# First expert layer of an eight-sublayer network on one core: GpSimd makes the first comparison of each half of the ternary weights, VectorE copies the turned row in 16 of 39 tiles

## The chip, the cores and the metric

The program runs on one core of one Trainium2 chip. The metric is the device time of one execution in microseconds, the median of several runs; lower is better. Engines: PE is TensorE, DVE VectorE, ACT ScalarE, POOL GpSimd, SP SyncE (it only issues DMAs here).

## The reference, cut to what matters

The network has four layers, each an attention and a feed-forward sublayer with a gated residual, over 2048 tokens (32 x 64) of width 256. Two sublayers matter here. The feed-forward sublayer of layer 0 is a mixture of 8 experts, of which each token takes two, beside a shared one. That of layer 1 is another mixture of 8 experts, whose weights are made ternary, matrix by matrix:

```
# layer 0, routed experts (inner width 176)
h = einsum('th,ehi->eti', x, w1); g = einsum('th,ehi->eti', x, w3)
y_all = einsum('eti,eih->eth', silu(h) * g, w2)

# layer 1, each of gate_w, up_w, down_w (512 x 256) of each of 8 experts
def weight_quant(w):
    scale = 1.0 / maximum(mean(abs(w)), EPS)
    return clip(round(w * scale), -1.0, 1.0) / scale
```

The quantised value is -1, 0 or 1 times the mean of the absolute values: 1 where w is above half the mean, -1 where it is below minus half the mean. The kernel makes it as (w > mean/2) - (w < -mean/2).

## The kernel before, in words

Layer 0's routed experts (`sorted_experts`, called by `layer0_experts`) sort the token rows by expert into 39 tiles of 128 rows (NT = 39) and then run one loop over the tiles, software-pipelined over three of its steps. All five engines run their own instruction stream, written out by hand and tied together by semaphores. Everything is computed in f32 split into a high and a low part (fp32r), so each product is three matmuls. In step j:

- SP fetches the row tile (`got`, ring of 7) and, by the table `LOADS_AT`, the raw weights of layer 1's experts (`tern_raw`, three slots).
- PE (`tensor`): up-projection of tile j (L1584, 6 matmuls into bank 2 or 3), turning of tile j-1's activation (L1598), turning of the rows of tile j+2 (`tensor_in`, L1542, into bank 0 or 1), down-projection of tile j-2 (L1610).
- ACT (`scalar`): silu of tile j (L1320), high part of the turned activation j-1 (L1326), high part of the turned row j+2 (`scalar_in`, L1343, `f_xT_hi`), the output y of tile j-2 (L1334, `f_y`), then `beside.scalar`.
- DVE (`vector`): silu times the second product, tile j (L1462, `f_act`), low part of the turned activation j-1 (L1467), then `vector_low(j+2)`: the places (L1418) and the low part of the turned row (L1419, `f_xT_lo`), then `beside.vector`.
- POOL (`gpsimd`): the scatter of y to its rows in memory, an indirect DMA for each tile (L1284), once s.out says that y is there.

Beside this loop runs the making of layer 1's ternary weights for four experts (`make_ternary`); each expert has three matrices of two halves, 128 x 512 each. It is spread over the tiles by `FIRST, PERIOD = 6, 7`: expert i has seven tiles from tile 6 + 7 i on. ACT sums absolute values in the first four of them (`beside_scalar`, L689: an activation and a read-out of the accumulator; two halves, one, two, one). In the fifth, PE adds the sums over partitions (`beside_tensor`, L700, four small matmuls into the bank that the turning uses next) and DVE makes mean, `above` and `below` (`beside_scale`, L706 to L709). From the sixth on, DVE makes the halves (`beside_vector`), two instructions each:

```
if x == 0:
    dve.tensor_scalar(to, src, below[:, m, n:n + 1], None, ALU.is_lt).then_inc(below_there, 1)
else:
    dve.wait_ge(below_there, 6 * i + 2 * m + h + 1)
    dve.scalar_tensor_tensor(to, src, above[:, m, n:n + 1], to, ALU.is_gt, ALU.subtract).then_inc(tern, 1)
```

(L717 and L720; `SHARES` gives five tiles one half each and splits the sixth half over the last two tiles.) The twelve halves of the later experts are made in layer 1's attention by the same functions.

When the loop is over, SP waits until the last scatters have landed, loads a bias row (L1715) and then fetches the outputs back (L1232) for the sum into the residual.

Of the kernel before, what the change touches and what calls it, by code (L numbers as in the profile page):

```python
# [8 lines left out]
ALU = mybir.AluOpType  # L9
# [10 lines left out]
P = 128  # L20
D = 256
DC = D // P
# [26 lines left out]
def build_program(nc, io):  # L49
    ctx = ExitStack()  # L50
    with ctx:
# [41 lines left out]
        bank = [ctx.enter_context(nc.psum_tensor(f"bank{i}", [P, 512], F32)) for i in range(8)]  # L93
# [558 lines left out]
        def make_ternary():  # L652


            w = Names()
# [3 lines left out]
            size, total, chain, below_there, tern = whole_sems[1:6]  # L659
# [3 lines left out]
            slot_of = (0, 1, 2, 0, 2, 0, 1, 2)  # L663
# [48 lines left out]
            def vector(dve, i, op):  # L712
# [5 lines left out]
                else:  # L718
                    dve.wait_ge(below_there, 6 * i + 2 * m + h + 1)
                    dve.scalar_tensor_tensor(to, src, above[:, m, n:n + 1], to, ALU.is_gt, ALU.subtract).then_inc(tern, 1)  # L720

            FIRST, PERIOD = 6, 7
            SHARES = ((0, 2), (2, 4), (4, 6), (6, 8), (8, 10), (10, 11), (11, 12))

# [13 lines left out]
            def beside_scale(dve, j, to):  # L738
                i, x = divmod(j - FIRST, PERIOD)
                if 0 <= i < 4 and x == 4:  # L740
                    vector_scale(dve, i, to)

            def beside_vector(dve, j):
                i, x = divmod(j - FIRST - 5, PERIOD)
                if 0 <= i < 4:
                    for op in range(*SHARES[x]):
                        vector(dve, i, op)

# [19 lines left out]
            w.beside_sync, w.beside_scalar, w.beside_tensor, w.beside_vector = beside_sync, beside_scalar, beside_tensor, beside_vector  # L768
            w.beside_scale = beside_scale
            w.behind_scalar = behind_scalar  # L770
# [3 lines left out]
        ternary = make_ternary()  # L774
# [272 lines left out]
        def sorted_experts(name, sublayer, split, turn, gate, before, done, g, experts, top, inner, shared_inner, router_args, at,  # L1047
# [23 lines left out]
                s.here0, s.here1, s.here2, s.here3, s.in_ps, s.hi, s.lo, s.up, s.silu, s.act, s.turn_ps, s.ahi, s.alo, s.down, s.out,  # L1071
                s.back0, s.back1, s.back2, s.back3, s.stat, s.acc
            ) = early.of("here0 here1 here2 here3 in_ps hi lo up silu act turn_ps ahi alo down out "
                         "back0 back1 back2 back3 stat acc")
            s.here, s.back = (s.here0, s.here1, s.here2, s.here3), (s.back0, s.back1, s.back2, s.back3)
# [158 lines left out]
            def gpsimd(pool):  # L1234
# [44 lines left out]
                for j in range(NT):  # L1279
                    pool.wait_ge(s.lo, j + 1)  # L1280
                    if j == 0:
                        pool.sem_clear(late.range)
                    pool.wait_ge(s.out, j + 1)
                    pool.indirect_dma_start(g.outputs, bass.IndirectOffsetOnAxis(ap=dest[:, j:j + 1], axis=0),  # L1284
                                            y_out[:, j % OUT_RING, :], None).then_inc(gone[j % OUT_RING], 16)

            def scalar(act):
# [27 lines left out]
                for j in range(NT + 2):  # L1315
# [5 lines left out]
                    if 1 <= j <= NT:  # L1321
# [4 lines left out]
                        act.activation(aT_hi[0:KR, i % 2].rearrange("p c n -> p (c n)"), bank[4 + i % 2][0:KR, 0:DC * P], ACT.Copy).then_inc(s.ahi, 1)  # L1326
                    if j + 2 < NT:
                        scalar_in(act, j + 2)
# [87 lines left out]
            def vector_low(dve, j):  # L1416
                dve.wait_ge(s.hi, j + 1)
                dve.tensor_copy(dest[:, j:j + 1], got[:, j % IN_RING, D:D + 1])  # L1418
                dve.tensor_tensor(xT_lo[:, j % 2].rearrange("p c n -> p (c n)"), bank[j % 2][:, 0:DC * P],  # L1419
                                  xT_hi[:, j % 2].rearrange("p c n -> p (c n)").bitcast(F32), ALU.subtract).then_inc(s.lo, 1)  # L1420
# [197 lines left out]
        def layer0_experts(before, done):  # L1618
# [48 lines left out]
            beside.behind_scalar = ternary.behind_scalar  # L1667
            beside.scale = ternary.beside_scale
            steps_at = {3: ("which",), 5: ("powers",), 7: ("series",), 9: ("weights",)}
# [2210 lines left out]
```

## Time and profile before

| | |
|---|---|
| median of 3 runs | 1132.63 us (1128.28 to 1133.96) |
| profiled execution | 1128.05 us, span 1126.2 us, mean granted clock 0.919 |
| busy share of the span | PE 81%, DVE 69%, ACT 54%, POOL 39% |
| loop over the 39 tiles | from 148.7 us (first L1584) to 240.6 us (end of the last scatter) |

How to read it: the engines' times overlap, so busy shares don't add up; what matters is which engine others wait for in each stretch. Times of single instructions in the trace are from start to end, and on DVE and ACT the next instruction can start some hundredths of a us before the end of the one ahead. PEld is TensorE's weight load. "<-" behind idle time names what ended it.

### The profile page before, as it was taken

To read this page: it belongs to the slowest core of one execution; us is meant where nothing else is said; L and a number is where in the kernel's file an instruction comes from. 1 tells how busy PE (TensorE), PEld (TensorE's weight loads), DVE (VectorE), ACT (ScalarE), POOL (GpSimd) and SP (SyncE) were. 2 spreads that over 40 slices of the span, in tenths; PEclk is the share of its full clock that TensorE was granted. 3 is DMA by queue.
4 is the path that set the end of the run, shared out by engine and by line. 5 is a ranking of instruction groups with operands and counts; after the bars stand their busy time and mean duration, and the time that the engine had idled before them with its cause. 6 is when DMAs were issued, how large, how long until landed. Compare 5 with 4: busy or idle time off the path is not lost. (4 is left out here: it accounts for less than half of the span.)

```text
span 1126.2 us, 20364 instructions
## 1 busy us (share of the span) xinstructions
PE 914.9 (81%) x5861; PEld 679.7 (60%) x5861; DVE 776.1 (69%) x2020; ACT 605.4 (54%) x1385; POOL 444.4 (39%) x518
## 2 busy tenths in 40 slices
PE   5867989968999776778779899977998898995187
PEld 4556779966777443444455556645777686763165
DVE  5756648867887687777768887656945354339987
ACT  3663347755443386777836566566134543433385
POOL 3176624440000104756436536531046666534400
PEclk9988989989999796999979999989999998985599
DMA  9954557765200031222190002011042532351001
GB/s 265 175 163 123 173 177 215 214 216 194 71 20 1 1 85 31 65 60 62 62 300 19 10 11 65 1 49 55 1 161 89 148 101 80 85 195 58 0 20 57
DMA packets 95971, 109.19 MB, mean 97 GB/s; under 512 B 14269, under 2 KB 85842, under 8 KB 95874
## 3 DMA queue, kind: packets, MB, share of 16 engines
q1 hardware_dynamic: 84162, 76.76, 23.7%
q0 software_dynamic: 11712, 31.20, 8.7%
q8 instruction: 53, 0.87, 0.3%
q14 instruction: 44, 0.36, 0.1%
HBM read 73.89 MB, written 34.03 MB: 96 GB/s over the span
## 5 line engine op out<-in xcount | busy, mean ns | idle before, releaser
L3125 POOL DMA_INDIRECT f_got<-f_tokens,f_places x54 | 54.9, 1016 | 61.9 <-DVE f_places L946 45.7
L3131 POOL DMA_INDIRECT f_outputs<-f_y,f_places x54 | 54.8, 1015 | 47.7 <-ACT f_y L3188 32.8
L3257 DVE TENSOR_TENSOR f_act<-f_silu,bank 128x256 f32<-128x256 f32 x54 | 22.7, 421 | 71.6 <-ACT f_silu L3174 51.5
L1284 POOL DMA_INDIRECT f_outputs<-f_y,f_places x39 | 41.7, 1068 | 56.1 <-ACT f_y L1334 32.7
L2087 POOL DMA_INDIRECT f_got<-f_tokens,f_places x39 | 41.2, 1057 | 55.3 <-DVE f_places L946 37.8
L2522 POOL TENSOR_TENSOR work<-work 128x512 f32<-128x512 f32 x32 | 32.7, 1052 | 71.3 <-ACT work L2572 71.3
L2095 POOL DMA_INDIRECT f_outputs<-f_y,f_places x39 | 38.7, 993 | 36.9 <-ACT f_y L2150 28.0
L2670 DVE TENSOR_REDUCE work<-bank 128x8 f32<-128x512 f32 x64 | 43.4, 679 | 12.4 <-PE bank L2768 12.2
L3347 PE MATMUL bank<-f_rhi,f_xT_hi 128*128 x108 | 44.3, 411 | 3.7 <-DVE f_xT_lo L3198 3.1
L2328 PE MATMUL bank<-tern,f_xq 128*128 x156 | 46.7, 428 | 0.5
L2674 DVE TENSOR_TENSOR work<-bank,work 128x512 f32<-128x512 f32 x64 | 44.3, 692 | 3.7 <-ACT work L2634 1.6
L2634 ACT ACTIVATE work<-work 128x512 f32<-128x512 f32 x64 | 40.3, 629 | 8.9 <-DVE work L2674 8.7
L2238 DVE TENSOR_TENSOR f_once<-f_relu,bank 128x512 f32<-128x512 f32 x39 | 26.7, 684 | 26.5 <-ACT f_relu L2131 18.4
L2809 PE MATMUL bank<-ident,work 128*128 128x128 f32 x256 | 42.8, 291 | 1.1 <-ACT work L2634 1.1
L3347 PE MATMUL bank<-f_rhi,f_xT_lo 128*128 x108 | 43.6, 404 | 0.0
L3347 PE MATMUL bank<-f_rlo,f_xT_hi 128*128 x108 | 43.5, 403 | 0.0
L3174 ACT ACTIVATE f_silu<-bank 128x256 f32<-128x256 f32 x54 | 20.9, 388 | 41.3 <-PE bank L3347 33.4
L258 POOL TENSOR_SCALAR ln_ve<-ln_mv 128x2 f32<-128x2 f32 x16 | 3.2, 199 | 101.2 <-DVE ln_mv L1484 93.2
L2802 PE MATMUL bank<-work 128*32 128x128 f32 x512 | 27.7, 288 | 18.8 <-ACT work L2637 18.6
L2637 ACT ACTIVATE work<-bank 128x512 f32<-128x512 f32 x64 | 38.0, 593 | 8.9 <-PE bank L2809 8.7
L223 DVE BATCH_NORM_STATS2 ln_stat<-resid 128x6 f32<-128x256 f32 x96 | 36.7, 414 | 3.6 <-DMA resid<-in_x 0.8
L3373 PE MATMUL bank<-f_rhi,f_aT_hi 128*128 x108 | 36.0, 333 | 3.9 <-DVE f_aT_lo L3261 2.2
(557 smaller groups left out, 3165.6 us busy)
## 6 DMA issues: line engine op xcount, KB each, us to landing
f_back<-f_outputs SPq DMA_DIRECT2D x21, 256.0 KB, 4.8
f_back<-f_outputs SPq DMA_DIRECT2D x10, 512.0 KB, 6.0
f_got<-f_sorted SPq DMA_DIRECT2D x39, 129.0 KB
f_sorted<-clear_row SPq DMA_DIRECT2D x1, 4992.0 KB, 28.5
raw<-in_L_ffn_w SPq DMA_DIRECT2D x24, 176.0 KB
tern_raw<-in_L_ffn_gate_w SPq DMA_DIRECT2D x8, 512.0 KB
tern_raw<-in_L_ffn_up_w SPq DMA_DIRECT2D x8, 512.0 KB
tern_raw<-in_L_ffn_down_w SPq DMA_DIRECT2D x8, 512.0 KB
```

What stands on the lines that cost most here:

```text
L1284: pool.indirect_dma_start(g.outputs, bass.IndirectOffsetOnAxis(ap=dest[:, j:j + 1], axis=0), y_out[:, j % OUT_RING, :], None).then_inc(gon ...
L2087: pool.indirect_dma_start(got[:, j, :], None, tokens, bass.IndirectOffsetOnAxis(ap=sorter.token[:, j:j + 1], axis=0)).then_inc(sent[j % FL ...
L2095: pool.indirect_dma_start(outputs, bass.IndirectOffsetOnAxis(ap=sorter.dest[:, j:j + 1], axis=0), y_out[:, j % OUT_RING, :], None).then_in ...
L2328: mm = pe.matmul(bank[b + j % 2][:, :], xq[:, j % 2, c, :], weights[:, ds(at + (m * MAT + c * I), I)], start=c == 0, stop=c == DC - 1)
L2634: act.activation(prob[:, x % 2, :], score[:, x % 2, :], ACT.Exp, scale=HD ** -0.5).then_inc(s.exp, 1)
L2637: act.activation(probT[:, (x - 1) % 2, :], TURN[:, :], ACT.Copy).then_inc(s.probT, 1)
L2670: dve.tensor_reduce(top[:, x % 2, :], got, AX.X, ALU.max).then_inc(s.top, 1)
L2674: dve.tensor_tensor(score[:, x % 2, :].rearrange("p (g k) -> p g k", g=GROUPS), got, top[:, x % 2, :].unsqueeze(2).to_broadcast([P, GROUPS ...
L2809: tp = pe.transpose(TURN[:, c * P:(c + 1) * P], prob[:, x % 2, c * P:(c + 1) * P], ident[:, :])
L3125: pool.indirect_dma_start(got[:, j % GATHERS, :], None, tokens, bass.IndirectOffsetOnAxis(ap=sorter.token[:, j:j + 1], axis=0)).then_inc(s ...
L3131: pool.indirect_dma_start(outputs, bass.IndirectOffsetOnAxis(ap=sorter.dest[:, j:j + 1], axis=0), y_out[:, j % OUT_RING, :], None).then_in ...
L3347: mm = pe.matmul(bank[2 + j % 2][:, :], x[:, j % 2, c, :], w[:, ds(where[j] + c * UP_COLS, UP_COLS)], start=n == 0, stop=n == 3 * DC - 1)
```

## The change

For the four experts of the loop, the first comparison (w below) moves from DVE to POOL (`gpsimd_below`, L725 of the changed kernel), one half behind each of six scatters, in POOL's steps 9 + 7 i to 14 + 7 i. It is written with a second operation, times 1.0. DVE makes the second comparison in its steps 12 + 7 i to 17 + 7 i (before: 11 + 7 i to 17 + 7 i), and waits there for POOL's. In the four tiles of each seven in which ACT sums weights, the high part of the turned row is no longer ACT's but DVE's: a copy out of the bank, a wait on that copy, then the places and the low part as before. A new semaphore `s.hi_taken` counts these copies. The later experts' halves, made in layer 1's attention, stay with DVE.

```diff
--- before.py
+++ after.py
@@ -719,8 +719,13 @@
                     dve.wait_ge(below_there, 6 * i + 2 * m + h + 1)
                     dve.scalar_tensor_tensor(to, src, above[:, m, n:n + 1], to, ALU.is_gt, ALU.subtract).then_inc(tern, 1)
 
+            def gpsimd_below(pool, i, m, h):
+                n = expert(i)
+                pool.wait_ge(chain, 3 * i + 3)
+                pool.tensor_scalar(half(w.tern[:, n], i, m, h), half(raw_m[slot_of[i]], i, m, h), below[:, m, n:n + 1], 1.0,
+                                   ALU.is_lt, ALU.mult).then_inc(below_there, 1)
+
             FIRST, PERIOD = 6, 7
-            SHARES = ((0, 2), (2, 4), (4, 6), (6, 8), (8, 10), (10, 11), (11, 12))
 
             def beside_scalar(act, j):
 
@@ -740,11 +745,20 @@
                 if 0 <= i < 4 and x == 4:
                     vector_scale(dve, i, to)
 
+            def beside_gpsimd(pool, j):
+                i, x = divmod(j - FIRST - 3, PERIOD)
+                if 0 <= i < 4 and x < w.PER:
+                    gpsimd_below(pool, i, x // 2, x % 2)
+
             def beside_vector(dve, j):
-                i, x = divmod(j - FIRST - 5, PERIOD)
-                if 0 <= i < 4:
-                    for op in range(*SHARES[x]):
-                        vector(dve, i, op)
+                i, x = divmod(j - FIRST - 6, PERIOD)
+                if 0 <= i < 4 and x < w.PER:
+                    vector(dve, i, 2 * x + 1)
+
+            def taken_by_vector(j):
+
+                i, x = divmod(j - 2 - FIRST, PERIOD)
+                return 0 <= i < 4 and x < 4
 
             LOADS_AT = {6: (0, 0), 7: (0, 1), 8: (0, 2), 11: (1, 0), 13: (1, 1), 15: (1, 2), 18: (2, 0), 20: (2, 1), 22: (2, 2),
                         24: (3, 0), 26: (3, 1), 28: (3, 2), 36: (4, 0), 37: (4, 1), 38: (4, 2)}
@@ -766,7 +780,7 @@
 
             w.sync, w.scalar, w.tensor, w.vector_scale, w.vector = sync, scalar, tensor, vector_scale, vector
             w.beside_sync, w.beside_scalar, w.beside_tensor, w.beside_vector = beside_sync, beside_scalar, beside_tensor, beside_vector
-            w.beside_scale = beside_scale
+            w.beside_scale, w.beside_gpsimd, w.taken_by_vector = beside_scale, beside_gpsimd, taken_by_vector
             w.behind_scalar = behind_scalar
             return w
 
@@ -1069,9 +1083,9 @@
             s = Names()
             (
                 s.here0, s.here1, s.here2, s.here3, s.in_ps, s.hi, s.lo, s.up, s.silu, s.act, s.turn_ps, s.ahi, s.alo, s.down, s.out,
-                s.back0, s.back1, s.back2, s.back3, s.stat, s.acc
+                s.back0, s.back1, s.back2, s.back3, s.stat, s.acc, s.hi_taken
             ) = early.of("here0 here1 here2 here3 in_ps hi lo up silu act turn_ps ahi alo down out "
-                         "back0 back1 back2 back3 stat acc")
+                         "back0 back1 back2 back3 stat acc hi_taken")
             s.here, s.back = (s.here0, s.here1, s.here2, s.here3), (s.back0, s.back1, s.back2, s.back3)
             was_sent, was_gone = scattered[-1][0:4], scattered[-1][4:]
             scattered.append(tuple(was_sent[r] + 16 * K * len(range(r, TILES, LINES)) * (r < LINES) for r in range(4))
@@ -1283,6 +1297,7 @@
                     pool.wait_ge(s.out, j + 1)
                     pool.indirect_dma_start(g.outputs, bass.IndirectOffsetOnAxis(ap=dest[:, j:j + 1], axis=0),
                                             y_out[:, j % OUT_RING, :], None).then_inc(gone[j % OUT_RING], 16)
+                    beside.gpsimd(pool, j)
 
             def scalar(act):
                 act.wait_ge(*before)
@@ -1324,7 +1339,7 @@
                         if i >= 2:
                             act.wait_ge(s.down, i - 1)
                         act.activation(aT_hi[0:KR, i % 2].rearrange("p c n -> p (c n)"), bank[4 + i % 2][0:KR, 0:DC * P], ACT.Copy).then_inc(s.ahi, 1)
-                    if j + 2 < NT:
+                    if j + 2 < NT and not beside.taken_by_vector(j + 2):
                         scalar_in(act, j + 2)
                     if j >= 2:
                         i = j - 2
@@ -1414,7 +1429,13 @@
                 dve.tensor_tensor(rlo[:, here], staging[:, n % STAGES, :], rhi[:, here].bitcast(F32), ALU.subtract).then_inc(p.lo_late, 1)
 
             def vector_low(dve, j):
-                dve.wait_ge(s.hi, j + 1)
+                if beside.taken_by_vector(j):
+                    dve.wait_ge(s.in_ps, j + 1)
+                    dve.wait_ge(s.up, j - 1)
+                    dve.tensor_copy(xT_hi[:, j % 2].rearrange("p c n -> p (c n)"), bank[j % 2][:, 0:DC * P]).then_inc(s.hi_taken, 1)
+                    dve.wait_ge(s.hi_taken, sum(beside.taken_by_vector(x) for x in range(j + 1)))
+                else:
+                    dve.wait_ge(s.hi, sum(not beside.taken_by_vector(x) for x in range(j + 1)))
                 dve.tensor_copy(dest[:, j:j + 1], got[:, j % IN_RING, D:D + 1])
                 dve.tensor_tensor(xT_lo[:, j % 2].rearrange("p c n -> p (c n)"), bank[j % 2][:, 0:DC * P],
                                   xT_hi[:, j % 2].rearrange("p c n -> p (c n)").bitcast(F32), ALU.subtract).then_inc(s.lo, 1)
@@ -1665,7 +1686,7 @@
             beside.bias_sync = lambda sp: layer1_weights.load_bias(sp)
             beside.context_sync = lambda sp: layer1_weights.load_context(sp, range(RING))
             beside.behind_scalar = ternary.behind_scalar
-            beside.scale = ternary.beside_scale
+            beside.scale, beside.gpsimd, beside.taken_by_vector = ternary.beside_scale, ternary.beside_gpsimd, ternary.taken_by_vector
             steps_at = {3: ("which",), 5: ("powers",), 7: ("series",), 9: ("weights",)}
             return sorted_experts("f0", 1, 0, 0, gates[:, 4:5], before, done, sorted0, EXPERTS, 2, L0_I, SHARED, (True, io["L0_ffn_gate_w"]),
                                   at, load_shared, load_routed, steps_at, beside)
```

DVE's rows in two steps of the loop that have both kinds of ternary work, before (L1462 is the product with silu, L1467, L1418 and L1419 as above, L717 and L720 the two comparisons):

```order
L1462 TENSOR_TENSOR f_act<-f_silu,bank 128x176
L1467 TENSOR_TENSOR f_aT_lo<-bank,f_aT_hi 88x256
L1418 CAST f_places<-f_got 128x1
L1419 TENSOR_TENSOR f_xT_lo<-bank,f_xT_hi 128x256
L717 TENSOR_SCALAR tern<-tern_raw_50,tern_table 128x512
L720 SCALAR_TENSOR_TENSOR tern<-tern_raw_50,tern_table,tern 128x512
```

and of the changed kernel, in a step in which ACT sums weights:

```order
L1483 TENSOR_TENSOR f_act<-f_silu,bank 128x176
L1488 TENSOR_TENSOR f_aT_lo<-bank,f_aT_hi 88x256
L1435 CAST f_xT_hi<-bank 128x256
L1439 CAST f_places<-f_got 128x1
L1440 TENSOR_TENSOR f_xT_lo<-bank,f_xT_hi 128x256
L720 SCALAR_TENSOR_TENSOR tern<-tern_raw_50,tern_table,tern 128x512
```

The number of rows is the same: the comparison behind the low part is gone, the copy L1435 stands in front of it.

POOL's rows in the same stretch of the changed kernel, where the comparisons of one expert end and those of the next begin (L1298 is the scatter; before, it stands there 39 times and nothing else):

```order
L1298 DMA f_outputs<-f_y,f_places 9088x256
L725 TENSOR_SCALAR tern<-tern_raw_51,tern_table 128x512
L1298 DMA f_outputs<-f_y,f_places 9088x256 x2
L725 TENSOR_SCALAR tern<-tern_raw_52,tern_table 128x512
L1298 DMA f_outputs<-f_y,f_places 9088x256
```

Six scatters of seven have a comparison behind them, the seventh has none.

## Rows read from the trace of the kernel before

**Rows 1.** The page: span, busy time of each engine.

```profile
span 1126.2 us, 20364 instructions
PE 914.9 (81%) x5861; PEld 679.7 (60%) x5861; DVE 776.1 (69%) x2020; ACT 605.4 (54%) x1385; POOL 444.4 (39%) x518
```

**Rows 2.** Windows: busy us, instructions in brackets, clock, DMA share, GB/s.

```profile
175.00:190.00 15.00, 14.38 (x109) 13.93 (x109) 13.24 (x42) 11.57 (x37) 7.06 (x7) 1.00 0.73 227
```

**Rows 3.** Timeline of one ordinary tile: start, duration, engine, line, operation.

```profile
176.64 0.33 DVE L1462 TENSOR_TENSOR f_act<-f_silu,bank 128x176 f32<-128x176 f32 x1
...
177.17 0.33 PE L1584 MATMUL bank<-f_rhi,f_xT_hi 128*128 x1
...
177.29 0.41 DVE L1419 TENSOR_TENSOR f_xT_lo<-bank,f_xT_hi 128x256 fp32r<-128x256 f32 x1
...
177.37 0.47 ACT L1334 ACTIVATE f_y<-bank,f_got 128x256 f32<-128x256 f32 x1 [0.29 <-issue]
...
177.62 0.47 DVE L717 TENSOR_SCALAR tern<-tern_raw,tern_table 128x512 bf16<-128x512 f32 x1
...
178.12 0.75 DVE L720 SCALAR_TENSOR_TENSOR tern<-tern_raw,tern_table,tern 128x512 bf16<-128x512 f32 x1
178.13 0.38 PE L1598 MATMUL bank<-ident,f_act 128*88 128x128 f32 x2
...
178.60 1.11 POOL L1284 DMA_INDIRECT f_outputs<-f_y,f_places  x1 [1.04 <-ACT f_y L1334]
...
179.28 0.33 PE L1584 MATMUL bank<-f_rhi,f_xT_hi 128*128 x1
...
179.44 0.41 DVE L1419 TENSOR_TENSOR f_xT_lo<-bank,f_xT_hi 128x256 fp32r<-128x256 f32 x1
...
179.48 0.48 ACT L1334 ACTIVATE f_y<-bank,f_got 128x256 f32<-128x256 f32 x1 [0.29 <-issue]
```

**Rows 4.** Timeline around one sum of the weights (L700).

```profile
185.62 0.33 PE L1584 MATMUL bank<-f_rhi,f_xT_hi 128*128 x1
...
186.03 0.47 ACT L1334 ACTIVATE f_y<-bank,f_got 128x256 f32<-128x256 f32 x1
...
186.91 0.20 ACT L689 ACTIVATION_READ_ACCUMULATOR tern<-tern_raw 128x1 f32 x1
...
187.37 0.58 PE L700 MATMUL bank<-tern_table,ones 128*128 128x3 f32 x4 [0.62 <-ACT tern L689]
...
188.98 0.33 PE L1584 MATMUL bank<-f_rhi,f_xT_hi 128*128 x1
```

**Rows 5.** Waits in 145 to 240 us: total us, times, longest us.

```profile
PEld bank L700 <- issue: 3.4, 4, 0.9
```

**Rows 6.** GpSimd's groups by shape, 512 wide: busy us, mean ns.

```profile
L2522 POOL TENSOR_TENSOR work<-work 128x512 f32<-128x512 f32 x32 | 32.7, 1052 | 71.3 <-ACT work L2572 71.3
L2941 POOL TENSOR_TENSOR f_rlo<-f_staging,f_rhi 128x512 fp32r<-128x512 f32 x21 | 26.6, 1295 | 0.0
...
L2937 POOL CAST f_rhi<-f_staging 128x512 fp32r<-128x512 f32 x21 | 12.6, 635 | 0.0
```

**Rows 7.** Timeline of GpSimd: two scatters in the loop.

```profile
183.03 1.47 POOL L1284 DMA_INDIRECT f_outputs<-f_y,f_places  x1 [1.17 <-DVE f_xT_lo L1419]
184.94 0.96 POOL L1284 DMA_INDIRECT f_outputs<-f_y,f_places  x1 [0.44 <-DVE f_xT_lo L1419]
```

**Rows 8.** Timeline of the loop's end and of what follows.

```profile
235.20 0.96 POOL L1284 DMA_INDIRECT f_outputs<-f_y,f_places  x1 [0.48 <-issue]
...
235.91 0.74 DVE L720 SCALAR_TENSOR_TENSOR tern<-tern_raw,tern_table,tern 128x512 bf16<-128x512 f32 x1
...
236.65 0.42 DVE L1467 TENSOR_TENSOR f_aT_lo<-bank,f_aT_hi 88x256 fp32r<-88x256 f32 x1
...
238.22 0.47 ACT L1334 ACTIVATE f_y<-bank,f_got 128x256 f32<-128x256 f32 x1 [0.60 <-PE bank L1610]
...
239.64 0.96 POOL L1284 DMA_INDIRECT f_outputs<-f_y,f_places  x1 [0.30 <-issue]
...
242.12 0.28 SPq L1715 DMA_DIRECT2D ctx_sb<-in_L_xattn_bg  x1
```

## The prediction

> **What bounds the kernel now.** I read the page first [rows 1]: one core, span 1126.2 us, TensorE busy 81% of it. That share is an average over many stages, so it says little about this change, which touches one loop of 39 tiles. The table of windows comes next [rows 2]: inside that loop TensorE is busy 14.38 of 15 us at full granted clock and VectorE 13.24 of 15, so both are nearly full, ScalarE less, GpSimd half empty. The timeline of one ordinary tile [rows 3] tells which of the two sets the pace. The first up-projection matmul of a tile starts at 177.17 and that of the next at 179.28: 2.11 us, with no gap in TensorE. VectorE's same instruction (L1419) comes at 177.29 and 179.44, a step of 2.15: it is full too, but what it makes is early. Its product L1462 ends at 176.97 and TensorE takes it at 178.13, 1.16 us later. So VectorE may fall 1.1 us behind before TensorE notices. TensorE is the bound, at 2.11 us a tile, and no edit on another engine can shorten that.
>
> What can be shortened are four places where TensorE does wait: the tile in which it adds up ScalarE's sums of the weights (L700). There a tile takes 188.98 - 185.62 = 3.36 us instead of 2.11 [rows 4], 1.25 us more. The table of waits gives the four together: the weight loads of L700 sat idle for 3.4 us [rows 5], 0.85 each. The other 0.4 of each is the four small matmuls themselves, which stay.
>
> **The change, part by part.** (1) ScalarE loses the copy of the turned row (L1343) in the four tiles in which it also sums weights. That seems to be four copies off a queue that is late, but only what stands ahead of the last sum without another wait behind it counts. The order on ScalarE is silu, copy, copy of the row, y (L1334), sums. y waits for TensorE's down-projection: in an ordinary tile it starts 179.48 - 177.17 = 2.31 us behind the tile's first matmul [rows 3]. In the fourth sum tile, which starts 2.11 ahead of 185.62, so at 183.51, y starts at 186.03 [rows 4], 2.52 behind. So at most 0.21 us of ScalarE's lateness is left at y; from there the last sum, its read-out (186.91) and L700 (187.37) follow rigidly. Removing four copies brings 0.21 us a time, four times 0.84 us. The rest of the wait stays, about 0.6 us a time.
>
> (2) VectorE gets 16 copies 128x256 out of PSUM, each followed by a wait on itself. No such copy on VectorE stands in the trace; the nearest row is L1419 of the same shape and with the same PSUM source, 0.41 us [rows 3]. A cast with one source can be somewhat shorter and can hardly be longer than it by more than the wait: 0.3 to 0.5, I take 0.42. It loses 24 comparisons L717 that hold it for 0.50 us each (177.62 to 178.12 [rows 3]). A copy tile thus costs VectorE 2.15 - 0.50 + 0.42 = 2.07 us, an ordinary ternary tile 1.65. Both are below 2.11; VectorE stops being full, and since TensorE had 1.16 us in hand this brings nothing by itself.
>
> (3) GpSimd gets 24 comparisons 128x512, f32 in and bf16 out, one behind each of six scatters out of seven. This is the unknown price. The trace has three rows of that width on GpSimd [rows 6]: a cast with one input 0.635 us, a two-input operation 1.052, a two-input subtraction to another type 1.295. The new one has one tensor input, so it is nearest to the cast; I take 0.70 and keep 0.64 and 1.30 as ends. The Trainium skill (GPSIMD Engine Reference, Engine selection) says that one-input operations run there at roughly line rate; the cast agrees with it, while its section on pitfalls of Q7 kernels puts bodies that compare and select at up to twice that unless they are unrolled, by which the price would be nearer to the second row.
>
> A scatter takes 0.96 us when nothing disturbs it, and back to back it comes 0.30 behind the one ahead [rows 7, 8]. With about 0.10 to start the comparison, GpSimd's cycle is 0.96 + 0.30 + 0.10 + p = 1.36 + p. With p = 0.70 that is 2.06, just under 2.11: it keeps up. The tipping point is p = 0.75.
>
> (4) VectorE's second comparison (L720) now waits for GpSimd, and behind it in VectorE's order stands all that TensorE needs. By rows 3: y ends at 177.84, its scatter starts at 178.60 and would end at 179.56; the comparison would be done at about 180.4. VectorE reaches its place in the next tile at 179.44 + 0.33 + 0.42 = 180.2. It waits 0.2 us, inside the 1.16 that TensorE has in hand. SP's waits on finished weights ask for groups that end in the same tiles as before, and SP runs seven tiles ahead.
>
> (5) The end of the loop has no such cover. The last comparison sits behind scatter 35, which starts at 235.20 [rows 8]: done at 236.16 + 0.10 + 0.70 = 236.96. VectorE's last L720, now at 235.91, moves to about 237.07; L1467 of the last tile follows 0.67 behind, at 237.74 instead of 236.65: 1.09 later. The last down-projection, the last y and the last scatter hang on it. Of this 0.19 was hidden: y of the last tile ends at 238.69 and would have let its scatter start 0.76 later, at 239.45, while the queue let it start at 239.64. The end of that scatter releases SP (242.12) and so the next stage. Cost: 0.90 us.
>
> Sum: -0.84 + 0.90 = +0.06 us, no change. For the profiled execution (1128.05 us) this gives 1128.1; the median of the runs shown is 1132.63, 4.6 above it, so the forecast is **1132.7 us**. A measurement of this kernel can tell about 0.5%, 5.7 us, from no change. The bounds of case A: with p = 0.64 and a copy of 0.3 the tail costs 0.85 and the sum is 0.0; if in the stretched tiles VectorE's fullness was the cause, some tenths come back: -0.5. With p = 0.9 GpSimd slips 0.15 a tile and the tail grows by 0.2 + 5 x 0.15 to 1.85: +1.0.
>
> **The rivals.**
>
> B, slower: GpSimd becomes the bound of the ternary tiles. With p = 1.05 its cycle is 2.41, 0.30 over the tile. The first wait of VectorE is 0.6, five tiles later it is 2.1, less the 1.16 in hand: TensorE loses 0.95 in a period, of which up to the 0.64 left of the wait at L700 may swallow a part, so 0.3 to 0.95, three times; the fourth period ends in the tail, which costs 1.09 + 0.35 + 1.5 - 0.19 = 2.75. With the gain of 0.84 taken off: +2.8 to +4.8, say +3.8. With p = 1.30 the same sum gives a slip of 0.55 a tile, three times 1.8 to 2.4, a tail of 4.3: +9 to +11. It decides from p of about 0.9 on. For it: the two-input rows, and that a comparison is not a cast. Against it: one input only.
>
> C, faster: the whole wait at L700 goes, 3.4 us, 1129.2. It needs y of the fourth sum tile not to hang on TensorE; rows 4 say that it does, so only if several sums slip ahead of it. The tail must cost nothing too.
>
> D, slower by contention: a scatter which starts while L720 runs takes longer. The one at 183.03 took 1.47 us instead of 0.96 [rows 7], with L720 running; the one at 178.60, which had L720 beside it for its first 0.27 us only [rows 3], took 1.11. L720 will now start just when GpSimd goes on to its next scatter, in 24 tiles. If each cost the full 0.51, the cycle is 2.57, as with p = 1.21 in B: +6 to +8, 1139.7. Against it: the scatter waits for y anyway, and by then half of L720 is over, so a cost of 0.15 to 0.3, which lands in A's upper part. The Trainium skill (SBUF, Who interferes with whom) states that a VectorE instruction with two SBUF inputs and a GpSimd instruction that reads SBUF exclude one another for the whole instruction, and that single-source VectorE operations from SBUF can do so too. The longer scatters over L720 agree. By that rule L720 would also hold back a comparison on GpSimd that meets it, which only happens once VectorE is a tile late.
>
> **How the numbers follow.** A 0.62, B 0.20, C 0.08, D 0.10. A spans 1132.2 to 1133.7 before the scatter of medians; C reaches to 1129.2, the middle of B and the lower part of D to 1139. The range 1129.0 to 1139.0 leaves out B's and D's upper parts and what the runs' own spread adds. Slower by over 5.7 us: B with p above 1.15, 0.07, and most of D's full price, 0.06, so 0.13. Faster by over 5.7 us: no case gives it (all four waits are 3.4), 0.03 for what I do not see. Within: 0.84.
>
> **What would show it.** Right: ordinary tiles keep a step of 2.11, also the 16 copy tiles; the four long tiles take about 3.15 instead of 3.36; L725 on GpSimd near 0.7; L720 preceded by idle time of VectorE of a few tenths, over 1 us in the last tile; the last scatter within some tenths of 239.6 less what came before. Wrong: L725 above 0.9, with tiles of TensorE above 2.11 that wait for L1483 or L1488 of VectorE (B); scatters of 1.4 us in most ternary tiles (D); long tiles near 2.5 (C).

## The result, and the profile after

The changed kernel takes 1165.99 us (median of 4 runs, 1165.12 to 1167.52), the kernel before 1131.33 in the same measurement: ratio 1.0312, 95% interval 1.0284 to 1.0340. It is 35 us slower where I had forecast no change, and outside my range.

The page of the changed kernel, its head:

```profile
span 1163.3 us, 20348 instructions
## 1 busy us (share of the span) xinstructions
PE 927.4 (80%) x5845; PEld 690.4 (59%) x5861; DVE 774.5 (67%) x2012; ACT 605.5 (52%) x1369; POOL 503.0 (43%) x542
```

Against [rows 1] the span is 37.1 us longer, VectorE has no more work than before and GpSimd 58.6 us more. A window in the ternary tiles, with the columns of [rows 2]:

```profile
180.00:195.00 15.00, 10.90 (x71) 9.50 (x70) 8.52 (x25) 8.51 (x26) 14.19 (x8) 0.96 0.49 143
```

TensorE is busy 10.9 us of 15 instead of 14.4, GpSimd 14.2 instead of 7.1. The bound has changed engines. Its groups in the loop (145 to 280 us; the last columns are busy us, mean ns, idle before):

```profile
L1298 POOL DMA_INDIRECT f_outputs<-f_y,f_places x39 | 51.4, 1317 | 32.0 <-ACT f_y L1349 22.8 <-DVE f_xT_lo L1440 5.3 <-issue 3.9
L725 POOL TENSOR_SCALAR tern<-tern_raw,tern_table 128x512 bf16<-128x512 f32 x24 | 48.2, 2010 | 1.1
```

One comparison takes 2.01 us, where I had taken 0.70 and set 1.30 as the upper end from [rows 6]. The scatter's mean went up as well, from 1.07 us in the loop before (0.96 for an undisturbed one) to 1.32. The timeline of one ternary tile, which answers to [rows 3]:

```profile
181.58 2.01 POOL L725 TENSOR_SCALAR tern<-tern_raw,tern_table 128x512 bf16<-128x512 f32 x1
...
182.17 0.42 PE L1605 MATMUL bank<-f_rhi,f_xT_hi 128*128 x1
...
183.63 0.75 DVE L720 SCALAR_TENSOR_TENSOR tern<-tern_raw,tern_table,tern 128x512 bf16<-128x512 f32 x1 [1.59 <-POOL tern L725]
183.76 1.54 POOL L1298 DMA_INDIRECT f_outputs<-f_y,f_places  x1 [0.17 <-issue]
184.30 0.33 DVE L1483 TENSOR_TENSOR f_act<-f_silu,bank 128x176 f32<-128x176 f32 x1
...
184.68 0.42 PE L1619 MATMUL bank<-ident,f_act 128*88 128x128 f32 x2 [1.29 <-DVE f_act L1483]
...
185.35 2.01 POOL L725 TENSOR_SCALAR tern<-tern_raw,tern_table 128x512 bf16<-128x512 f32 x1
...
185.94 0.42 PE L1605 MATMUL bank<-f_rhi,f_xT_hi 128*128 x1
```

GpSimd repeats after 185.35 - 181.58 = 3.77 us: comparison 2.01, 0.17 to the scatter, scatter 1.54, 0.05. TensorE repeats after 185.94 - 182.17 = 3.77 too. The chain is to be seen row by row: the comparison ends at 183.59, VectorE, which had idled 1.59 us for it, starts L720, only then comes to L1483, and TensorE takes that product after 1.29 us of idleness. The table of waits, 145 to 280 us:

```profile
DVE tern L720 <- POOL tern L725: 41.4, 24, 2.4
...
PEld bank L1619 <- DVE f_act L1483: 22.8, 18, 2.6
```

All 24 of VectorE's second comparisons wait for GpSimd, 41.4 us in total. Not every tile of TensorE takes 3.77 us: in each period of seven two do, the next two take over 4.1, the one behind them 2.9 to 3.1. L720 keeps its step of 3.77, and a whole period takes 23.9 us (its first L720 starts at 179.85, the next period's at 203.71) where it took 16.0. From the first tile to the last the loop takes 112.5 us (148.66 to 261.20) where it took 85.0 (148.73 to 233.77): 27.5 us. Behind the last tile come the last ternary steps and scatters, which answer to [rows 8]:

```profile
270.21 0.75 DVE L720 SCALAR_TENSOR_TENSOR tern<-tern_raw,tern_table,tern 128x512 bf16<-128x512 f32 x1 [2.44 <-POOL tern L725]
...
270.88 0.41 DVE L1488 TENSOR_TENSOR f_aT_lo<-bank,f_aT_hi 88x256 fp32r<-88x256 f32 x1
...
274.34 0.96 POOL L1298 DMA_INDIRECT f_outputs<-f_y,f_places  x1 [1.19 <-ACT f_y L1349]
...
276.82 0.28 SPq L1736 DMA_DIRECT2D ctx_sb<-in_L_xattn_bg  x1
```

The last scatter starts 13.1 us behind the last tile's first matmul instead of 5.9, another 7.3. A part of this is TensorE's clock. The windows of the end, of the kernel before and of the changed one:

```profile
235.00:240.00 5.00, 3.05 (x22) 2.34 (x20) 1.82 (x5) 3.53 (x11) 3.24 (x4) 1.00 0.25 89
```

```profile
265.00:270.00 5.00, 2.19 (x10) 1.58 (x8) 1.33 (x3) 1.26 (x3) 4.78 (x3) 0.55 0.13 44
270.00:275.00 5.00, 1.64 (x6) 1.35 (x6) 1.12 (x3) 1.96 (x7) 3.34 (x4) 0.50 0.15 52
```

TensorE, which had been busy for 2.4 and 3.6 of 5 us in the two windows before (255 to 265 us), is granted 0.50 of full speed there, the lower of its two levels (1.2 GHz), and 1.00 (2.4 GHz) at the end of the loop before. The last down-projection takes 1.64 us (271.43 to 273.07) instead of 0.97 (237.21 to 238.18), 0.7 of the 7.3 us. SP goes on at 276.82 instead of 242.12: 34.7 us. Of the 37.1 us by which the spans differ, all but 2.4 are there by then.

### The profile page after: what moved, and what is told of

Same layout as the page of the kernel before. It is cut to its first block and busy times, and to the rows that moved or that the text cites. A ratio compares the mean times of both kernels' runs of the same rounds, so it can differ in the third digit from the quotient of the medians.

```text
span 1163.3 us, 20348 instructions
## 1 busy us (share of the span) xinstructions
PE 927.4 (80%) x5845; PEld 690.4 (59%) x5861; DVE 774.5 (67%) x2012; ACT 605.5 (52%) x1369; POOL 503.0 (43%) x542
## 5 line engine op out<-in xcount | busy, mean ns | idle before, releaser
L3152 POOL DMA_INDIRECT f_outputs<-f_y,f_places x54 | 56.2, 1041 | 50.2 <-ACT f_y L3209 37.4
L1298 POOL DMA_INDIRECT f_outputs<-f_y,f_places x39 | 51.4, 1317 | 32.0 <-ACT f_y L1349 22.8
L720 DVE SCALAR_TENSOR_TENSOR tern<-tern_raw,tern_table,tern 128x512 bf16<-128x512 f32 x48 | 35.9, 748 | 41.7 <-POOL tern L725 41.4
L2116 POOL DMA_INDIRECT f_outputs<-f_y,f_places x39 | 39.3, 1008 | 38.6 <-ACT f_y L2171 30.5
L725 POOL TENSOR_SCALAR tern<-tern_raw,tern_table 128x512 bf16<-128x512 f32 x24 | 48.2, 2010 | 1.1
L2349 PE MATMUL bank<-tern,f_xq 128*128 x146 | 43.4, 422 | 2.5 <-issue 1.9
```

Source lines behind the costliest of these rows:

```text
L725: pool.tensor_scalar(half(w.tern[:, n], i, m, h), half(raw_m[slot_of[i]], i, m, h), below[:, m, n:n + 1], 1.0, ALU.is_lt, ALU.mult).then_i ...
L2116: pool.indirect_dma_start(outputs, bass.IndirectOffsetOnAxis(ap=sorter.dest[:, j:j + 1], axis=0), y_out[:, j % OUT_RING, :], None).then_in ...
L2349: mm = pe.matmul(bank[b + j % 2][:, :], xq[:, j % 2, c, :], weights[:, ds(at + (m * MAT + c * I), I)], start=c == 0, stop=c == DC - 1)
L3152: pool.indirect_dma_start(outputs, bass.IndirectOffsetOnAxis(ap=sorter.dest[:, j:j + 1], axis=0), y_out[:, j % OUT_RING, :], None).then_in ...
```

## The experiments

There were eleven runs, of ten kernels (`sum_later_again` is `sum_later` once more). `copies_only`, `gpsimd_only`, `forms_a` and `sum_later` ran on a chip on which the kernel before takes 1132.24 us; `forms_b`, `arith`, `short_second` and `three_of_six` on one on which it takes 1087.15; `narrow`, `sum_later_again` and `sum_and_copies` on a third, 1084.73. I compare each with the kernel before on its own chip. The changed kernel itself has no run on the two faster chips, so where I set a run there beside its 3.1%, a ratio or a difference is carried from one chip to another. What speaks for this is that the loop's rows agree: an undisturbed tile takes 2.11 us in every trace, the comparison 2.01. Lines that a diff leaves out are marked `...`.

**Which half of the change costs.** `copies_only` gives both comparisons back to VectorE, in the steps of the kernel before, and keeps the 16 copies of the turned row there:

```diff
 def beside_gpsimd(pool, j):
-    i, x = divmod(j - FIRST - 3, PERIOD)
-    if 0 <= i < 4 and x < w.PER:
-        gpsimd_below(pool, i, x // 2, x % 2)
+    pass
...
 def beside_vector(dve, j):
-    i, x = divmod(j - FIRST - 6, PERIOD)
-    if 0 <= i < 4 and x < w.PER:
-        vector(dve, i, 2 * x + 1)
+    i, x = divmod(j - FIRST - 5, PERIOD)
+    if 0 <= i < 4:
+        for op in range(*SHARES[x]):
+            vector(dve, i, op)
```

> The 16 copies of the turned row stay with VectorE; both comparisons are VectorE's, in the steps of the kernel before. Theory 1 (GpSimd's comparison of 2.01 us sets the pace of the ternary tiles): the 33 us go, the time is within 2 us of before; the four sum tiles take 3.04 to 3.15 us (3.36 before), three copy tiles of each period load VectorE with 2.15 + 0.42 = 2.57 us, which eats up to 1.4 us against 1.16 in hand, so up to 0.3 us a period may come back as stalls. Theory 2 (the copies on VectorE, with their wait, cost a good part of it): at least 8 us slower than before, with TensorE waiting for L1483-like products in copy tiles.

`gpsimd_only` keeps the comparisons and gives the copies back to ScalarE:

```diff
 def taken_by_vector(j):
-    i, x = divmod(j - 2 - FIRST, PERIOD)
-    return 0 <= i < 4 and x < 4
+    return False
```

> Only GpSimd's comparisons; the copies of the turned row stay with ScalarE. Theory 1: as the changed kernel, 33 to 35 us slower than before, 24 comparisons of 2.01 us and a step of 3.77 us in five tiles of seven. Theory 2: at least 8 us faster than the changed kernel.

Measured: 1133.51 us, ratio 1.0013 (0.9991 to 1.0035), and 1166.01 us, ratio 1.0278 (1.0244 to 1.0311). The copies are neutral within 0.4%, and the comparisons alone bring 2.8 of the 3.1% (the two intervals overlap): theory 2 falls. The copies did what step (1) of the prediction says. From one first matmul to the next the four sum tiles of `copies_only` take 3.04, 3.16, 3.11 and 3.14 us (before: 3.23, 3.36, 3.36, 3.35), where I had worked out 3.15. The copy itself is measured, of `copies_only`'s groups in 150 to 245 us:

```profile
L1436 DVE CAST f_xT_hi<-bank 128x256 fp32r<-128x256 f32 x16 | 6.6, 410 | 0.0
```

0.41 us, against my 0.42 with the wait.

**What makes the comparison slow.** `forms_a` and `forms_b` put another instruction in its place for each of the four experts i of the loop (the lines in short form):

```diff
+if i == 0: ins = pool.tensor_scalar(to, src, limit, None, ALU.is_lt)              # forms_a
+if i == 1: ins = pool.tensor_scalar(to, src, -0.01, 1.0, ALU.is_lt, ALU.mult)
+if i == 2: ins = pool.tensor_scalar(to, src, limit, 1.0, ALU.mult, ALU.mult)
+if i == 3: ins = pool.tensor_copy(to, src)
+if i == 0: ins = pool.tensor_scalar(to, src, 1.0, -1.0, ALU.min, ALU.max)         # forms_b
+if i == 1: ins = pool.tensor_scalar(src, src, limit, 1.0, ALU.is_lt, ALU.mult)
+if i == 2: ins = pool.tensor_scalar(to, src, 2.0, None, ALU.mult)
+if i == 3: ins = pool.tensor_tensor(to, src, src, ALU.subtract)
```

> The changed kernel with four forms of GpSimd's instruction, one for each of the four experts of the loop: comparison alone without the second operation; comparison with a constant instead of the pointer operand; two multiplications with the pointer; a plain copy to bf16. This changes the first comparison's values, so the output is not the reference's. If the second operation makes it slow: the first is near 1 us. If the pointer operand does: the second is near 1. If the comparison does: the third is near 1. If the conversion to bf16 does: all stay near 2, the copy too; else the copy is 0.64.

> The changed kernel with four more forms on GpSimd, one for each expert: minimum and maximum with constants; the comparison written in place as f32; one multiplication without a second operation; a subtraction of two tensors to bf16. The output is not the reference's. If only comparisons are slow: minimum and maximum near 0.7, the comparison near 2.0 whatever its output type, one multiplication 0.65 to 0.70, the subtraction near 1.05. If it is the output type that makes the comparison slow: the second form is near 1.

GpSimd's groups by shape of `forms_a` (L727 is the first form, L733 the fourth):

```profile
L729 POOL TENSOR_SCALAR tern<-tern_raw 128x512 bf16<-128x512 f32 x6 | 11.6, 1940 | 0.3
L727 POOL TENSOR_SCALAR tern<-tern_raw,tern_table 128x512 bf16<-128x512 f32 x6 | 9.5, 1583 | 0.3
L731 POOL TENSOR_SCALAR tern<-tern_raw,tern_table 128x512 bf16<-128x512 f32 x6 | 4.2, 697 | 0.3
L733 POOL CAST tern<-tern_raw 128x512 bf16<-128x512 f32 x6 | 3.7, 618 | 0.0
```

and of `forms_b` (again L727, L729, L731, L733 in the order of the forms):

```profile
L729 POOL TENSOR_SCALAR tern_raw<-tern_raw,tern_table 128x512 f32<-128x512 f32 x6 | 12.1, 2014 | 0.3
L731 POOL TENSOR_SCALAR tern<-tern_raw 128x512 bf16<-128x512 f32 x6 | 9.1, 1517 | 0.2
L733 POOL TENSOR_TENSOR tern<-tern_raw 128x512 bf16<-128x512 f32 x6 | 6.3, 1050 | 0.2
L727 POOL TENSOR_SCALAR tern<-tern_raw 128x512 bf16<-128x512 f32 x6 | 3.8, 625 | 0.2
```

Two arithmetic operations with the same pointer operand, the same tensors and the same types take 0.70 us, minimum and maximum 0.63, the copy to bf16 0.62. The comparison takes 2.01 with the pointer, 1.94 with a constant and 2.01 with f32 out. So neither the pointer nor the conversion is to blame, but the comparison is, beside two arithmetic operations in the same form. What I did not expect: an instruction without a second operation is slow too, 1.59 us for the comparison and 1.52 for a plain multiplication, more than twice the two multiplications. The forecasts of "near 1" for the first form and 0.65 to 0.70 for the single multiplication were wrong. Written without its "times 1.0" the comparison would still be too long: TensorE's tiles beside the first form take 3.35 us, not 2.11. The two kernels as a whole, one execution each (1142.41 and 1103.13 us), mix four forms and show nothing more.

**Was the price the only fault?** `arith` is the change at the price that the prediction took, with one word altered:

```diff
-                                   ALU.is_lt, ALU.mult).then_inc(below_there, 1)
+                                   ALU.mult, ALU.mult).then_inc(below_there, 1)
```

> The changed kernel with a multiplication in the place of GpSimd's comparison, same operands (the first comparison's values are wrong, so the output is not the reference's). This is the change at the price of 0.70 us that the prediction took. If the price was its only fault, the time is within 1 us of before. If the hold of L720 on the scatter counts (1.54 instead of 0.96), GpSimd's cycle is 0.70 + 0.17 + 1.54 + 0.05 = 2.46, 0.35 over a tile: part of it in VectorE's reserve, 2 to 8 us slower than before.

Measured: 1087.17 us against 1087.15, ratio 1.0001 (0.9983 to 1.0019). With 0.70 us the forecast of no change holds, within 2 us. Its GpSimd rows, however, show a cycle that I had not taken:

```profile
183.83 0.70 POOL L725 TENSOR_SCALAR tern<-tern_raw,tern_table 128x512 bf16<-128x512 f32 x1
184.69 1.55 POOL L1298 DMA_INDIRECT f_outputs<-f_y,f_places  x1 [0.17 <-issue]
186.29 0.70 POOL L725 TENSOR_SCALAR tern<-tern_raw,tern_table 128x512 bf16<-128x512 f32 x1
```

2.46 us, not 2.06: the scatter takes 1.55. GpSimd falls 0.35 us behind in each of six tiles, and VectorE waits 9.5 us for it in total, but its reserve and the seventh tile without a comparison take up nearly all of that. Not so at the end: the last scatter starts 8.2 us behind the last tile's first matmul, 2.3 more than before, where I had worked out 0.90. From the eleventh tile's first matmul to the start of the last scatter the two traces show 72.6 us, before 69.9. So a ratio so near to 1 is partly luck; a loss of up to 2 us is within the interval.

**The hold on the scatter.** `short_second` cuts VectorE's L720 to 8 columns in the loop:

```diff
+                    if i < 4:
+                        to, src = to[:, 0:8], src[:, 0:8]
                     dve.scalar_tensor_tensor(to, src, above[:, m, n:n + 1], to, ALU.is_gt, ALU.subtract).then_inc(tern, 1)
```

> The changed kernel, but VectorE's second comparison in the loop covers 8 of the 512 columns (504 columns of each half of four experts keep only the first comparison, so the output is not the reference's). Theory 1 (GpSimd's own cycle sets the pace, and its scatter is held up by the wide L720 that starts when the comparison ends): scatters 0.96 to 1.1 us instead of 1.54, a step of 2.01 + 0.17 + 0.96 + 0.05 = 3.19 us instead of 3.77, 24 times 0.57 = 13 to 14 us faster than the changed kernel, about 1152. Rival (the 1.54 comes from the comparison on GpSimd itself, such as a slow start of a scatter behind it): scatters stay at 1.54 and the time within 2 us of the changed kernel's 1166.

Measured: 1107.65 us against 1087.15, ratio 1.0173 (1.0123 to 1.0222). Its GpSimd rows:

```profile
187.77 2.02 POOL L727 TENSOR_SCALAR tern<-tern_raw,tern_table 128x512 bf16<-128x512 f32 x1
189.96 1.05 POOL L1300 DMA_INDIRECT f_outputs<-f_y,f_places  x1 [0.17 <-issue]
191.05 2.01 POOL L727 TENSOR_SCALAR tern<-tern_raw,tern_table 128x512 bf16<-128x512 f32 x1
```

The comparison is what it was, the scatter 1.05 us instead of 1.54, the cycle 3.28 instead of 3.77, and TensorE's tiles 3.26 instead of 3.77. The changed kernel's loss of 3.1% becomes 1.7%. By the traces, from the eleventh tile to the last scatter: 69.9 us before, 104.2 changed, 92.2 here, so about two thirds of the loss stay without the hold that L720 puts on the scatter. The parts don't simply add up, though. With the hold and a short instruction (`arith`) there is no loss to be told; the hold costs only because the long comparison has already used up the time. The rival, a slow start of a scatter behind a comparison, falls but for 0.09 us: 1.05 instead of 0.96, and 22 of the 24 scatters behind a comparison in `narrow`, further down, take 1.04 or 1.05 too.

**Half the dose.** `three_of_six` leaves GpSimd the first half of each matrix and gives the second back to VectorE:

```diff
-                if 0 <= i < 4 and x < w.PER:
-                    gpsimd_below(pool, i, x // 2, x % 2)
+                if 0 <= i < 4 and x < w.PER and x % 2 == 0:
+                    gpsimd_below(pool, i, x // 2, 0)
...
+                    if x % 2:
+                        vector(dve, i, 2 * x)
...
                     vector(dve, i, 2 * x + 1)
```

> The changed kernel with only every second of GpSimd's comparisons (12), the others back with VectorE. Theory 1: two tiles cost GpSimd 3.77 + 0.96 + 0.30 = 5.03 us where TensorE needs 4.22, 0.81 a pair, 12 pairs, less VectorE's reserve of about 1.1 us a period: 4 to 9 us slower than before. A rival in which each wait of VectorE for GpSimd is itself the cost gives half of the changed kernel's loss, 16 to 17 us.

Measured: 1097.11 us against 1087.15, ratio 1.0096 (1.0063 to 1.0130), 10 us slower: a third of the loss for half of the comparisons, just above the 4 to 9 of theory 1 and far from the 16 to 17 of the rival. That fits a cost of only the part that is over TensorE's pace. The theory had left out the tail, where the last scatter starts 8.8 us behind the last tile's first matmul (before: 5.9), and the following; of GpSimd and of VectorE:

```profile
184.09 2.54 POOL L731 TENSOR_SCALAR tern<-tern_raw,tern_table 128x512 bf16<-128x512 f32 x1
```

```profile
183.70 1.06 DVE L726 SCALAR_TENSOR_TENSOR tern<-tern_raw,tern_table,tern 128x512 bf16<-128x512 f32 x1
```

Here the second comparison (L726 of this kernel, 0.75 us elsewhere) runs into GpSimd's first. Both get longer, by 0.31 and 0.53 us. The scatter that still runs when this L726 starts (until 184.04) is not what lengthens it: at 194.85 and 213.20 an L726 starts as far into a scatter with no comparison behind it, and takes 0.75. In the changed kernel the two never meet, since one waits for the other.

**A quarter of the width.** `narrow` gives GpSimd 128 of 512 columns and VectorE the other 384:

```diff
-                pool.tensor_scalar(half(w.tern[:, n], i, m, h), half(raw_m[slot_of[i]], i, m, h), below[:, m, n:n + 1], 1.0,
+                pool.tensor_scalar(half(w.tern[:, n], i, m, h)[:, 0:128], half(raw_m[slot_of[i]], i, m, h)[:, 0:128], below[:, m, n:n + 1], 1.0,
...
+                    dve.tensor_scalar(half(w.tern[:, expert(i)], i, m, h)[:, 128:HALF], half(raw_m[slot_of[i]], i, m, h)[:, 128:HALF],
+                                      below[:, m, expert(i):expert(i) + 1], None, ALU.is_lt).then_inc(first_there, 1)
+                    dve.wait_ge(first_there, 6 * i + x + 1)
                     vector(dve, i, 2 * x + 1)
```

> The changed kernel, but GpSimd compares 128 of the 512 columns and VectorE the other 384. If GpSimd's time is by the column, 2.01 us becomes 0.19 + 1.82 / 4 = 0.65, its cycle 0.65 + 0.17 + 1.54 + 0.05 = 2.41 with L720's hold, so as with the multiplication: within 2 us of before. If most of the 2.01 is fixed, as slow as the changed kernel, 30 us over before.

Measured: 1091.12 us against 1084.73, ratio 1.0061 (1.0032 to 1.0090), 6 us slower and not within 2. GpSimd's part is near what was foreseen, 0.72 to 0.84 us in 19 of 24 cases and 0.93 to 1.14 in the others, so the 2.01 is mostly by the column. But VectorE again has both comparisons, 0.98 + 0.42 (copy) + 0.44 + 0.67 = 2.5 us in a copy tile. Of its timeline, GpSimd's rows and VectorE's:

```profile
183.16 1.05 POOL L1303 DMA_INDIRECT f_outputs<-f_y,f_places  x1 [0.26 <-issue]
...
186.38 0.75 POOL L726 TENSOR_SCALAR tern<-tern_raw,tern_table 128x128 bf16<-128x128 f32 x1
```

```profile
183.67 0.78 DVE L758 TENSOR_SCALAR tern<-tern_raw,tern_table 128x384 bf16<-128x384 f32 x1
...
186.58 0.41 DVE L758 TENSOR_SCALAR tern<-tern_raw,tern_table 128x384 bf16<-128x384 f32 x1
```

The same instruction of VectorE takes 0.78 us at 183.67, 0.51 us into a scatter (183.16 to 184.21), and 0.41 beside GpSimd's comparison. Not every scatter does this: the four L758 that start 0.42 to 0.59 us into one take 0.61 to 0.87, the seven that start earlier in one or near its end take 0.41 or 0.42. A tile of 2.92 us comes back, in front of a sum tile of 3.10 (`copies_only`: 2.19 and 3.16), and the tail is 1.9 us longer than before. How the 6 us divide between the fuller schedule of VectorE and these longer instructions no run here separates.

**A version that beats both.** The four waits of 0.85 us before L700 [rows 5] need no change of engines. VectorE makes its first comparison one tile later than it makes the scales, so the sum can wait for ScalarE in the tile behind. `sum_later` is the kernel before with:

```diff
 def beside_tensor(pe, j, to):
     i, x = divmod(j - FIRST, PERIOD)
-    if 0 <= i < 4 and x == 4:
+    if 0 <= i < 4 and x == 5:
         tensor(pe, i, to)
 def beside_scale(dve, j, to):
     i, x = divmod(j - FIRST, PERIOD)
-    if 0 <= i < 4 and x == 4:
+    if 0 <= i < 4 and x == 5:
         vector_scale(dve, i, to)
```

> Kernel before, with TensorE's sum over partitions and VectorE's scales one tile later (sixth of seven instead of fifth); nothing else moves. If the wait for ScalarE's last sum is what the four long tiles lose, the wait of 0.85 us before each L700 goes: long tiles 2.5 instead of 3.36 us, the whole 3 to 3.5 us faster (0.3%). If the wait is only moved (VectorE's first comparison now follows the scales at once), within 1 us of before.

> The sum over partitions one tile later, once more, to see whether 0.3 to 0.4% is more than the spread between measurements. If the four waits before L700 are what it gains, the ratio is 0.996 to 0.998; if the first result was luck of one chip, 0.999 to 1.001.

Measured: 1127.70 us against 1132.24, ratio 0.9958 (0.9943 to 0.9973), and on another chip 1081.93 against 1084.73, ratio 0.9976 (0.9957 to 0.9995). The table of waits of the second, 145 to 245 us:

```profile
PEld bank L700 <- issue: 0.4, 2, 0.2
```

3.4 us of waiting became 0.4, and the sum tiles take 2.50 to 2.69 us instead of 3.36. That is the 3 us that moving work between engines was not needed for. The gain is small, 0.2 to 0.4%, but both intervals lie below 1.

Its neighbour `sum_and_copies` adds the copies on VectorE to it, and is otherwise the sum of `sum_later` and `copies_only`.

> The sum one tile later and, beside it, the copies of the turned row on VectorE in the tiles in which ScalarE sums weights; both comparisons on VectorE. If ScalarE's lateness was only felt at L700, the copies add nothing more, and VectorE's 2.57 us in three tiles of each period cost up to 1 us: 0 to 2 us slower than the sum alone. If ScalarE still delays other products, up to 1 us faster than it.

Measured: 1087.00 us against 1084.73, ratio 1.0028 (1.0008 to 1.0048): 5 us slower than the sum alone (1081.93), not 0 to 2. With both comparisons and a copy VectorE is loaded with 2.57 us in three tiles running, and in each later period two of TensorE's tiles take 2.8 and 2.6 us, and the sum tile 2.9 to 3.2 instead of 2.5 to 2.7. The likely reason is that in `copies_only` the long sum tile gives VectorE time to recover: it has its product ready 0.9 to 1.1 us before TensorE takes it at the start of a later period's copy tiles, here 0.62, and in the tile behind that 0.4 to 0.6 us, here 0.13. I had priced this reserve too high. No run tests that reading by itself.

## Why the prediction was wrong

The step of the prediction that failed is (3), the price of GpSimd's comparison. I took 0.70 us and bounded it by 0.64 and 1.30, from a cast, a two-input operation and a subtraction. It is 2.01, half as much again as the upper end. I argued by the number of input tensors; what counts is the operation and the form: with two multiplications the same instruction takes 0.70, as `arith` shows, and the ratio to before is then 1.0001. The cycle that step (3) worked out for a price of 0.70, 2.06 us, was wrong too: in `arith` it is 2.46, because L720 holds the scatter. The sentence on the Trainium skill that I had set aside, from the GPSIMD Engine Reference's pitfalls for Q7 kernels, pointed the right way: it puts bodies that compare and select at up to twice the cost unless they are unrolled. The runs show a factor of 2.9, 2.01 to 0.70 us, more than the section's, and in this built-in instruction, where the section speaks of kernels of one's own.

Rival B described what happened, at 0.20 and with a price of +3 to +11: GpSimd over TensorE's pace, VectorE's second comparison waiting, TensorE waiting for L1483 and L1488, from p of about 0.9 on. Its mechanism was right, its size wrong because p lay outside its bounds and the hold on the scatter came on top.

Rival D, the hold of L720 on the scatter, was real in full: 1.53 to 1.54 against 0.96 us in all 24 scatters behind a comparison in the changed kernel, about 1.05 with a short L720. I had put it at 0.15 to 0.3 in case A, arguing that the scatter waits for y anyway; it doesn't once GpSimd is late. About 0.09 of the 0.58 us is not the hold but the comparison ahead. Together with p it makes the cycle 3.77. The Trainium skill (SBUF, Who interferes with whom) speaks of an exclusive lock, by which the one that comes second is fully blocked. The held scatters fit a full block: those that start 0.1 us or more into L720 end 0.83 to 0.92 us behind its end in 43 of 44 cases (the kernel before and the changed one), whether 0.6 or 0.2 us of it was left. But the same section infers that a tensor_tensor, which has two inputs like L720, does not hold the making of a DMA's descriptors, and here it is a DMA issued on GpSimd that is held; the measurement decides. Of two that meet in `three_of_six` both are lengthened, by less than the other's whole length, which a full block of the second alone does not give. A single-source comparison on VectorE, which the section says can use the shared ports, is not lengthened by one on GpSimd in `narrow`.

Step (1) held: 0.21 us a sum tile worked out, 0.19 to 0.25 measured in `copies_only`. Rival C, the whole wait gone by the copies, fell with it. Step (2) held: the copy takes 0.41 us. The gaps of GpSimd, in step (3), were 0.17 and 0.05 us, not 0.30 and 0.10. Step (4), a wait of 0.2 us inside TensorE's reserve, became one of 1.7 on average (41.4 us in 24). Step (5), the tail as the place without cover, was right in kind: there the changed kernel loses 7.3 us, and `arith`, at p = 0.70, 2.3 in place of the 0.9.

What the prediction should have drawn from its own rows: no comparison of a tensor with a limit stood anywhere on GpSimd in the trace of before, and the three rows of the same width already spread by a factor of two. Bounds from such rows are no bounds for another operation, and the tipping point, 0.75 to 0.9 us, lay so close to the value taken that a surprise could only go one way.

## What to carry to other kernels

Before work moves to an engine that stands in a loop with the bound, write down that engine's cycle in the loop (all its instructions, the gaps, and what holds them up) and compare it with the bound's pace: below it, or above it by what reserve and free turns take up (2.46 against 2.11 us in `arith`), the move shows in no ratio here; beyond that the excess is paid in turn after turn. An operation's price on GpSimd is to be measured for that very operation and form. And where an engine waits for a late sum, look first whether the sum can be asked for later; two changed digits gained 0.2 to 0.4%, the move between engines nothing even at its hoped-for price.

## What the runs showed of the hardware

- GpSimd, 128 x 512, f32 in: copy to bf16 0.62 us, minimum and maximum 0.63, two multiplications with a pointer operand 0.70, subtraction of two tensors 1.05, one multiplication without a second operation 1.52, comparison alone 1.59, comparison and multiplication 1.94 to 2.01. With 128 columns the last takes 0.81 on average.
- A scatter on GpSimd that starts 0.1 us into VectorE's operation with two inputs in SBUF (L720, 0.75 us) takes 1.47 us, and 1.53 or 1.54 behind a comparison, instead of 0.96; one that starts when 0.2 us of L720 are left takes 1.02. One that starts 0.13 us ahead of L720 is not held (0.96).
- Directly behind a comparison a scatter that nothing holds takes 1.05 us, not 0.96.
- It works the other way too. VectorE's small L708 (128 x 3, 0.17 us before) takes 0.59 in the changed kernel where it falls into a scatter with a comparison behind it:

```profile
195.06 1.53 POOL L1298 DMA_INDIRECT f_outputs<-f_y,f_places  x1 [0.17 <-issue]
...
196.03 0.59 DVE L708 TENSOR_SCALAR tern_table<-tern_table 128x3 f32<-128x3 f32 x1
```

It does so three times out of three. In `three_of_six` the same instruction stands as far into a scatter of 1.54 us three times, with another scatter behind it, and takes 0.17 each time; why is open.
